# Copies of the rank keys dealt 14 to ACT and 10 to DVE, and the lists of the latents' block in another order

## The reference

```
xn = layernorm(x)                                   # both branches start from it; below, x is xn
c_q     = x @ W_dq                                  # latents of the queries, 64 wide
query_c = c_q @ W_uq                                # 8 heads x 64
query_r = pope(c_q @ W_qr, angles_q)                # 8 heads x 32; pope = softplus, then a rotation
idx     = top_k(I, 96)                              # 96 positions per query; all of the last 64 are among them
key_r   = pope((x @ W_kr)[bi, idx], angles_k)       # rotated by the RANK of a key in the list, not its position
scores  = (query_c . key_c + query_r . key_r) * scale
attn    = softmax(scores);  s = (attn @ value) @ W_out

y = x                                               # the gate's branch, 2 layers
y = y + local_attention(shift_token(y)) @ wo
h = (h - mean) / sqrt(var + 1e-5) * lg + lb         # h = shift_token(y)
a, g = split(h @ w1 + b1)                           # 2 x 341 wide
y = y + (a * gelu(g)) @ w2 + b2
gate = silu(y)                                      # after the last layer

out = x_in + s * gate
```

## Time and profile before

| | |
|---|---|
| median of 3 runs | 1229.78 us (1229.46 to 1231.81) |
| profiled execution, own time | 1229.35 us |
| its span | 1227.6 us |
| PE busy | 961.4 us (78%) |
| DVE busy | 833.0 us (68%) |
| ACT busy | 622.6 us (51%) |
| POOL busy | 268.8 us (22%) |
| mean granted clock of PE | 0.913 |
| start of the four passes through `bridge` (ACT's first load) | 181.2, 477.8, 775.8, 1072.1 us |
| copies out of PSUM in `bridge` | 48 on ACT of 594 ns, 48 on DVE of 682 ns (medians, all four passes) |

### The profile page before, as it was taken

One profiled execution on the slowest core, in us unless ns is written; L12 is line 12 of the kernel. 1 busy time (PEld: TensorE's weight loads), 2 busy tenths in 40 slices (PEclk: granted clock), 3 DMA queues, 4 the chain that ended last, 5 costly groups with the idle time before them and its releaser, 6 DMA issues. The chain is left out here.

```text
span 1227.6 us, 22767 instructions
## 1 busy us (share of the span) xinstructions
PE 961.4 (78%) x8572; PEld 560.7 (46%) x8580; DVE 833.0 (68%) x1651; ACT 622.6 (51%) x1637; POOL 268.8 (22%) x196
## 2 busy tenths in 40 slices
PE   1788979678588988768749897867875889796785
PEld 0345363467325345256623535336652353634673
DVE  0653977599454596769826289669973539775995
ACT  1165457345535564635633656554462654563455
POOL 0230740001032281000103247000102307400000
PEclk9999988799789997889969999789987999887998
DMA  7010100664001000166201000046510101005640
GB/s 285 1 31 1 26 17 20 136 112 79 8 3 32 9 23 19 57 130 111 42 9 27 6 9 23 19 101 123 94 27 5 31 1 26 11 26 132 116 79 8
DMA packets 235754, 61.88 MB, mean 50 GB/s; under 512 B 220945, under 2 KB 231697, under 8 KB 235281
## 3 DMA queue, kind: packets, MB, share of 16 engines
q1 hardware_dynamic: 235632, 60.28, 22.5%
HBM read 45.45 MB, written 7.47 MB: 43 GB/s over the span
## 5 line engine op out<-in xcount | busy, mean ns | idle before, releaser
L1906 ACT ACTIVATE KC<-PS 96x1024 bf16<-96x1024 f32 x64 | 65.1, 1018 | 133.4 <-PE PS L1672 133.4
L1672 PE MATMUL PS<-onehot,CX 128*96 128x512 bf16 x320 | 83.9, 393 | 34.9 <-DVE onehot L1997 27.1
L1997 DVE TENSOR_SCALAR onehot<-idxb,consts 128x1024 bf16<-128x1024 f16 x160 | 79.3, 547 | 36.8 <-DMA idxb<-idx_scratch 21.2
L800 ACT ACTIVATE S<-PS,nmax 128x128 f32<-128x128 f32 x256 | 90.1, 399 | 12.5 <-DVE nmax L1047 12.5
L2020 DVE TENSOR_REDUCE xnT<-PS 32x64 f32<-32x192 f32 x256 | 90.7, 354 | 3.8 <-ACT V L1914 0.7
L1892 POOL TENSOR_TENSOR SC<-SC,jrec 128x1280 f32<-128x1280 f32 x12 | 28.4, 2367 | 278.4 <-DVE jrec L2035 278.4
L1682 PE MATMUL PS<-onehot,XR 128*96 128x128 bf16 x1280 | 85.8, 224 | 3.1 <-DVE KR L2003 2.7
L1682 PEld LDWEIGHTS PS<-onehot,XR 128*96 128x96 bf16 x1280 | 79.5, 126 | 15.4 <-DVE KR L2003 10.6
L2003 DVE CAST KR<-PS 96x1024 bf16<-96x1024 f32 x64 | 78.0, 1218 | 9.5 <-PE PS L1682 8.4
L788 ACT ACTIVATE sq<-PS 128x512 f32<-128x512 f32 x64 | 38.1, 595 | 78.2 <-PE PS L448 57.6
L447 PE MATMUL PS<-hT,wts 128*128 128x512 f32 x128 | 68.5, 616 | 10.8 <-ACT hT L770 5.7
(11 more groups left out here) (235 smaller groups left out, 2202.4 us busy)
## 6 DMA issues: line engine op xcount, KB each, us to landing
idxb<-idx_scratch SPq DMA_DIRECT2D x64, 256.0 KB, 3.7
q3c<-q_scratch SPq DMA_DIRECT2D x96, 96.0 KB, 2.6
q3r<-q_scratch SPq DMA_DIRECT2D x96, 96.0 KB, 2.6
v<-v SPq DMA_DIRECT2D x56, 128.0 KB, 2.3
q_scratch<-q3s SPq DMA_DIRECT2D x16, 384.0 KB, 2.8
wts<-weights_dram SPq DMA_DIRECT2D x1, 4825.5 KB, 20.5
consts<-consts_dram SPq DMA_DIRECT2D x1, 2691.5 KB, 9.0
x_next<-x_dram SPq DMA_DIRECT2D x5, 256.0 KB, 4.7
```

The lines of the kernel that those rows point to most:

```text
L800: last = op(S[:, i, h, :], reg[:, h // 4, (h % 4) * P:(h % 4 + 1) * P], ACT.Exp, bias=nmax[:, i, h:h + 1], accum_out=rsum[:, i, h:h + 1])
L1672: last = mm(k.Z[0:96, e, :], k.CX[:, j, :], onehot[:, n % 2, j, e * 512:(e + 1) * 512], start=(j == 0), stop=(j == i))
L1906: op(KC[:, i % 2, :, :].rearrange("p t (g r) -> p t g r", g=GR)[:, :, :, q * RB:(q + 1) * RB], k.Z[0:96, :, :].rearrange("p a (r g t) -> p ...
L1997: last = ve.tensor_scalar(onehot[:, n % 2, j, :], idxb[:, n % 2, :], C("iota")[:, j:j + 1], None, ALU.is_equal)
```

## The change

Only the order of the calls in `bridge` changes, on PE, ACT and DVE, and with it which engine makes which of the 24 copies: before each engine made 12, alternating; after it ACT makes 14 and DVE 10. No instruction is added or removed otherwise, and no wait is written anew; the lists of SP and POOL, and the other two blocks, are the same. Since two lines are added above it, DVE's lines are numbered two higher after it (L1480 becomes L1482, L1519 becomes L1521 and so on).

```diff
--- before.py
+++ after.py
@@ -1312,40 +1312,40 @@
                               start=(j == 0), stop=(j == 2))
                 last.then_inc(rU.full, 1)
 
+            turn(0)
             rope_queries(0)
-            turn(0)
+            take_off(0, 0)
             turn(1)
-            take_off(0, 0)
+            take_off(0, 1)
+            content_queries(0)
+            turn(2)
+            take_off(1, 0)
             centre()
-            take_off(0, 1)
-            take_off(1, 0)
+            take_off(1, 1)
+            rope_queries(1)
+            take_off(2, 0)
+            turn(3)
             variance()
-            rope_queries(1)
-            take_off(1, 1)
-            turn(2)
-            turn(3)
-            take_off(2, 0)
-            content_queries(0)
             take_off(3, 0)
             take_off(2, 1)
+            content_queries(1)
+            turn(4)
+            take_off(3, 1)
             up(0)
-            take_off(3, 1)
-            turn(4)
+            take_off(4, 0)
             turn(5)
+            take_off(4, 1)
             up(1)
-            take_off(4, 0)
             take_off(5, 0)
-            content_queries(1)
+            turn(6)
             take_off(5, 1)
-            take_off(4, 1)
             up(2)
-            turn(6)
+            take_off(6, 0)
             turn(7)
+            take_off(6, 1)
+            take_off(7, 0)
             down()
-            take_off(7, 0)
-            take_off(6, 0)
             take_off(7, 1)
-            take_off(6, 1)
 
         @block.scalar
         def _(act):
@@ -1427,41 +1427,43 @@
 
             exp_ln_table()
             shift_x1()
+            rank_part(0, 0)
             magnitude(0)
-            rank_part(0, 0)
             exponential(0)
             logarithm(0)
+            keep_content(0)
+            rank_part(1, 1)
             square_centred()
-            rank_part(0, 2)
+            content_hi(0)
+            rank_part(2, 0)
+            magnitude(1)
+            rank_part(2, 1)
+            exponential(1)
             log_variance()
-            rank_part(1, 1)
+            rank_part(2, 2)
             inverse_std()
-            magnitude(1)
-            exponential(1)
-            rank_part(2, 0)
+            keep_content(1)
             logarithm(1)
+            gelu(0)
+            rank_part(4, 1)
+            content_mid(0)
             rope_hi(0)
-            rank_part(3, 1)
-            rank_part(2, 2)
-            gelu(0)
-            rank_part(4, 0)
-            keep_content(0)
-            rope_mid(0)
+            rank_part(4, 2)
+            content_hi(1)
             gelu(1)
             rank_part(5, 1)
-            keep_content(1)
-            content_hi(0)
-            rank_part(4, 2)
+            rope_mid(0)
+            rank_part(6, 0)
+            rope_hi(1)
+            rank_part(5, 2)
             gelu(2)
-            rope_hi(1)
-            content_hi(1)
-            content_mid(0)
+            rank_part(6, 1)
+            rank_part(7, 0)
             rope_mid(1)
             content_mid(1)
-            rank_part(6, 0)
+            rank_part(6, 2)
             rank_part(7, 1)
             gate()
-            rank_part(6, 2)
             exp_ln_table()
 
         @block.vector
@@ -1552,41 +1554,39 @@
                                         ALU.add).then_inc(a.x2_ready, 1)
 
             shift_x1()
+            rank_part(0, 1)
+            rank_part(0, 2)
             rank_part(1, 0)
-            rank_part(0, 1)
             softplus(0)
+            turn_rope(0)
+            group_content(0)
+            rank_part(1, 2)
             local_products(0)
-            turn_rope(0)
             local_sums(0)
-            rank_part(1, 2)
+            rank_part(3, 0)
+            content_rest(0)
+            sum_rope(0)
+            rank_part(3, 1)
             norm_hidden()
-            sum_rope(0)
-            rank_part(3, 0)
-            rank_part(2, 1)
+            rank_part(4, 0)
+            group_content(1)
+            rank_part(3, 2)
             softplus(1)
+            hidden(0)
+            turn_rope(1)
+            rank_part(5, 0)
             rope_rest(0)
-            turn_rope(1)
-            rank_part(3, 2)
-            hidden(0)
+            content_rest(1)
+            hidden(1)
+            sum_rope(1)
+            rope_lo(0)
             local_products(1)
-            sum_rope(1)
-            rank_part(5, 0)
-            group_content(0)
-            rank_part(4, 1)
-            hidden(1)
-            rope_lo(0)
-            rank_part(5, 2)
-            local_sums(1)
-            content_rest(0)
-            group_content(1)
+            rope_rest(1)
             hidden(2)
-            rope_rest(1)
-            content_rest(1)
             content_lo(0)
             rope_lo(1)
-            rank_part(7, 0)
             content_lo(1)
-            rank_part(6, 1)
+            local_sums(1)
             add_hidden()
             rank_part(7, 2)
```

## The result

The changed kernel takes 1252.16 us (1242.51 to 1256.01, 4 runs) against 1230.32 us: 1.0164 times as long, 95% interval 1.0099 to 1.023. I had forecast 1224.5, faster. Its profiled execution has a span of 1254.2 us against 1227.6.

The account below looks back on a forecast made before the run. No engine is full; each of four bridges ends through PE's front, DVE's stretch, then ACT's tail. Gains of 3 x 1.4 + 1.1 = 5.3 us from 1229.35 give 1224.05, 1224.5 for the median; range 1219.5 to 1229.3.

Parts of the forecast that it names:

- the PE part: PE's front of a bridge: clock as before, turn(4) ends at 21.1 us, DVE's last stretch starts about 0.7 us earlier.
- Rival 3: PE's front: a missed wait for a copy brings longer half clock, so the kernel is slower, 1231.6 us; chance 0.08.
- The price of half clock: PE's front of a bridge: each us more at half clock costs 0.5 us.
- The tail: ACT's end of a bridge: gate and table load without a copy between, 3.21 us against 3.70, gain 0.5 per bridge.
- DVE's run: DVE from its copy after turn(4) to add_hidden's end: 15.44 us against 15.73, 0.3 shorter.
- The second chain: PE's down-projection ends 0.05 us before DVE reaches add_hidden; delayed hand-overs could lengthen a bridge by 0 to 0.6 us.
- The laying-out: All three engine lists set end to end at profiled prices: ACT's end at 39.72 us against 41.04, difference 1.3.
- DMA: SP's last q3s store in a bridge begins earlier, after content_lo(1) at about 34.5 us against 36.1; no cost.

Follow-up runs that it names:

- the tall form: Changed kernel with turns, rope queries and content queries over all 128 rows (zero rows added): 1207.51 us; same edit in the kernel before: 1219.26 us.
- the second trace of the changed kernel: The changed kernel run again as it is: 1250.68 us, ratio 1.0203 to the kernel before.
- the form with the tall unused products: Changed kernel with 8 unused bf16 products of 128x512 over all 128 rows put first in PE's bridge list: 1224.54 us, ratio 0.9956 to the kernel before.

## Why the prediction was wrong

**The step that failed** is the first sentence of the PE part: "For the first 10 us the clock is at 1.2 GHz in both kernels", and "I count it as before, so turn(4) ends at 21.1". I took the clock's course from the old trace as if it were given, and moved the work underneath it; but the work makes the clock. It was 1.2 GHz for 16 to 37 us, turn(4) ended at 28.6 in the fourth bridge, and each bridge lost 0.8 to 9.5 us. The rows to see it stood in the earlier trace rows: 32*128 and 64*128 up to 7.4 us, then 128*128, and the rise at 10.2 among them. The fall at 17.0 came behind two turns, the wait of 0.36, a take_off and half a content query. I leaned to the wait; but the third bridge of the same trace has the same instructions with a wait of 0.46, and no fall:

```profile
793.12 0.39 PE L1274 MATMUL PS<-XR,consts 128*128 128x512 bf16 x1 [0.46 <-ACT XR L1357]
```

```profile
788.80:815.00 26.20, 21.92 (x51) 6.84 (x49) 23.57 (x34) 20.27 (x32) 0.00 (x0) 1.00 0.18 60
```

So neither that wait nor those low products alone made it fall. The turns and queries were low there as well; with all of them tall (the kernel before in that form) the short stretch came in none of the four bridges.

**Rival 3** had the outcome (half clock for longer in the front, two of four bridges, 1231.6) at 0.08, by the wrong mechanism: missed waits for copies. In the long bridges PE missed none while the clock was at half. Its own price, 0.5 us for each us more at half clock, gives for 23.8 us more (37.4 against 13.6) 11.9, less the 1.9 that the order is worth 10.0; measured 9.4 and 9.5. That agreement is in part luck: in bridge 2, with 2.6 us more at half clock, the same sum gives a gain of 0.6, and 0.8 was lost. My argument against it, that the old order had one wait and one short stretch, took the wait for the cause.

**The price of half clock** was a second, smaller fault. From the tall form to the form as it is, a bridge of the new order lengthens by about 0.41 us for each us more at half clock ((50.87 - 36.75) / (37.5 - 3.4)), one of the old order by 0.26 ((41.36 - 38.69) / (13.6 - 3.4)); both are estimates from two bridges each. That may be because PE bounds more of the new order's front; no run shows it. So even at the clock that I had assumed the gain was smaller: the first bridge of the second trace of the changed kernel had 13.6 us at half clock, as much as before (10.2 and 3.4), and took 40.8, 0.6 less than before, where I had forecast 1.4 less.

**The tail**: 3.21, right; alone it is worth half of its 0.5, since the copy still waits for PE's last take_off. **DVE's run**: 15.44 forecast; with the clock out of the way it took 15.68 without a wait (1079.17 to 1094.85 in the tall form of the changed kernel), and the two copies moved to ACT are worth 1.0 us in a bridge. **The second chain**: down ended 0.4 us before add_hidden began there (1090.97 + 2.74 against 1094.10), no bound. **The laying-out**, given half clock to 3.4 us, says 36.6 and 38.5 for the two orders (the lower ends on record for the two tall forms); measured 36.75 and 38.66. So with the clock near full the sums of the lists were good to 0.2 us and the gain of the order is real. The clock under them took it and more: 20.8 us and the 7.6 that the order is worth there (4 x 1.9), over five times the forecast gain. **DMA** cost nothing that shows: PE's next stage begins 0.63 us after ACT's end (1140.09 against 1139.46), as before (0.66).

The Trainium skill (TensorE: Matmul & The Clock Gate, part 1) lets the clock go by how busy the engine is. The runs differ: 37.37 busy us of 37.40 at half clock in the changed kernel, full clock with 26.0 of 29.2 when the same products are tall.

Open: whether it is the rows of the array or the rows read from memory that count, which no run here separates; why the same front brings a fall of the clock in three bridges of the kernel before and not in its third; and why one bridge of the same execution stays at half clock for 16 us and another for 37, with the same instructions at the same distances for the first 15.

## What to carry to other kernels

When a change reorders TensorE's work, look at the rows that each product uses in the profile's form column (32*128, 64*128, 128*128) beside the granted clock, and keep full-height products together early in a stage that begins at half clock; or pad short contractions with zero rows, which cost PE no time here (at full clock a turn ahead of a take_off takes 1.06 us from start to start over 32 rows, 1127.04 to 1128.10 in the changed kernel, and 0.95 over 128, 1065.99 to 1066.94 in its tall form) and took 45 us off the changed kernel and 11 off the one before. Never carry the clock of the old trace over to a new order: price the sum at both levels, and let the distance between them into the range.

## What the runs showed of the hardware

- A low product next to a tall one costs more than two tall ones: a take_off takes 0.32 us from start to start ahead of a turn over 32 rows (1085.48 to 1085.80) and 0.22 ahead of one over 128 (1065.77 to 1065.99).
- Two low products on different rows of the array ran at the same time (the rows above, 184.85 beside 183.18 to 185.47).
- Rows that are zero in one of the two operands counted for the clock: with them added it rose 3.4 us after the start, where it had stayed at half for 37.5.
- The clock fell with PE busy without a gap: 6.80 of 6.80 us at full clock, then half (1071.8 to 1082.0 in the form with the tall unused products).
